# The last layer of a four-layer graph network: fetch, softmax and sums of the attention in one stage, by blocks of 112 edge tiles

## The reference

```python
def _L3_gnn_ref(x, W_u, b_u, W_v, src, dst):
    s_u = x @ W_u.T + b_u
    s_v = x @ W_v.T
    e = s_u[src] + s_v[dst]
    e = jnp.where(e >= 0, e, 0.2 * e)
    m = jax.ops.segment_max(e, dst, num_segments=n_nodes)
    e_exp = jnp.exp(e - m[dst])
    denom = jax.ops.segment_sum(e_exp, dst, num_segments=n_nodes)
    probs = e_exp / denom[dst]
    xh = x.reshape(n_nodes, head_dim, num_heads)
    msg = xh[src] * probs[:, None, :]
    out = jax.ops.segment_sum(msg, dst, num_segments=n_nodes)
    return out.reshape(n_nodes, dim)
...
h = jnp.maximum(_layernorm(x, axis=-1), 0.0)
x = x + _L3_gnn_ref(h, L3_gnn_W_u, L3_gnn_b_u, L3_gnn_W_v, src, dst)
```

## Time and profile before

| what | us |
|---|---|
| median of 3 runs | 10575.17 |
| lowest and highest run | 10565.06, 10585.32 |
| profiled execution, its time | 10629.75 |
| profiled execution, span from first to last instruction | 10628.0 |
| of it: w_uv and T4 | 8391 to 8495 |
| fetch of the last layer | 8495 to 9783 |
| softmax, two halves | 9783 to 9889, 9889 to 9996 |
| sums, with 14 us of opening | 9996 to 10583 |
| division, residual, output | 10583 to 10628 |

### The profile page before, as it was taken

One profiled execution on the slowest core, in us unless ns is written; L12 is line 12 of the kernel. 1 busy time (PEld: TensorE's weight loads), 2 busy tenths in 40 slices (PEclk: granted clock), 3 DMA queues, 4 the chain that ended last, 5 costly groups with the idle time before them and its releaser, 6 DMA issues. The chain is left out here.

```text
span 10628.0 us, 131026 instructions
## 1 busy us (share of the span) xinstructions
PE 5936.1 (56%) x24674; PEld 4756.4 (45%) x24675; DVE 4831.8 (45%) x13494; ACT 2018.0 (19%) x5480; POOL 5350.6 (50%) x5364
## 2 busy tenths in 40 slices
PE   4788886674656666645554454454455633222376
PEld 2687775553544444433333343333343432222254
DVE  6344446776544444435554233343333411112777
ACT  2111111783322222200000000010000300000276
POOL 3555552000068888876665666646666056664000
PEclk9777877997877777766666677777777655555699
DMA  4554556563067777754444333323333156665265
GB/s 148 163 158 157 166 160 208 181 200 106 2 113 105 104 105 105 104 120 142 142 142 130 91 89 91 89 82 87 91 90 90 60 165 196 188 195 151 77 200 181
DMA packets 848105, 1375.07 MB, mean 129 GB/s; under 512 B 112503, under 2 KB 501429, under 8 KB 847749
## 3 DMA queue, kind: packets, MB, share of 16 engines
q0 software_dynamic: 315328, 634.04, 27.1%
q1 hardware_dynamic: 398452, 575.30, 16.7%
q10 hardware_dynamic: 133968, 161.50, 4.8%
HBM read 949.47 MB, written 420.93 MB: 129 GB/s over the span
## 5 line engine op out<-in xcount | busy, mean ns | idle before, releaser
L1028 POOL DMA_INDIRECT regionB<-table,gather_rows x2352 | 2283.5, 971 | 1400.9 <-POOLq L1025 765.4
L1028 POOL DMA_INDIRECT regionC<-table,gather_rows x1568 | 1508.6, 962 | 861.2 <-issue 453.4
L1760 POOL DMA_INDIRECT scatter_sums<-regionC,idx x880 | 1383.7, 1572 | 306.2 <-issue 247.5
L1128 PE MATMUL ps_p<-regionB,hot 128*128 x3520 | 998.5, 443 | 846.4 <-DVE regionC L1189 511.6
L1128 PEld LDWEIGHTS ps_p<-regionB,hot 128*128 128x128 f32 x3520 | 782.9, 226 | 1035.6 <-issue 903.7
L1496 PE MATMUL ps_p<-regionA 128*128 128x266 f32 (+1 forms) x3520 | 848.4, 394 | 336.1 <-PEq L1491 216.2
L1128 PE MATMUL ps_p<-regionC,hot 128*128 x1760 | 621.7, 498 | 561.2 <-issue 487.5
L1965 PE MATMUL psS<-dst_scores,regionA 128*128 x1760 | 393.3, 362 | 897.3 <-PEq L1963 616.8
L1496 PEld LDWEIGHTS ps_p<-regionA 128*128 128x128 f32 x3520 | 653.2, 190 | 531.1 <-DVE regionC L974 194.2
L1965 PEld LDWEIGHTS psS<-dst_scores,regionA 128*128 128x128 f32 x1760 | 383.6, 330 | 907.1 <-issue 907.1
L1128 PEld LDWEIGHTS ps_p<-regionC,hot 128*128 128x128 f32 x1760 | 419.6, 249 | 763.3 <-issue 704.1
(11 more groups left out here) (309 smaller groups left out, 8503.1 us busy)
## 6 DMA issues: line engine op xcount, KB each, us to landing
regionA<-edge_rows SPq DMA_DIRECT2D x880, 256.0 KB, 3.3
edge_rows<-regionB SPq DMA_DIRECT2D x196, 512.0 KB
edge_rows<-regionC SPq DMA_DIRECT2D x392, 256.0 KB
regionC<-srcrow_d SPq DMA_DIRECT2D x220, 256.0 KB
scatter_sums<-zero_rows ACTq DMA_DIRECT2D x8, 6400.0 KB, 41.6
regionA<-scatter_sums ACTq DMA_DIRECT2D x49, 1024.0 KB
regionB<-table,gather_rows POOLq DMA_INDIRECT x2352
regionB<-rrow_d ACTq DMA_DIRECT2D x110, 256.0 KB
```

Source lines behind the costliest of these rows:

```text
L1028: g.indirect_dma_start(out=rows_of(b * per + j), out_offset=None, in_=table, in_offset=bass.IndirectOffsetOnAxis(ap=idx[:, column:column + ...
L1128: x = te.matmul(ps[(u.c * VG + j) % NB], hot[:, b, 2 * j + k, :], at_tile(G, slot[j] * 2 + k), start=k == 0, stop=k == 1)
L1760: g.indirect_dma_start(out=scat, out_offset=bass.IndirectOffsetOnAxis(ap=idx[:, b, j:j + 1], axis=0), in_=sums[:, b, j, :], in_offset=None ...
```

## The change

`attention_in_blocks` takes the place of `attention_fetch3`, both calls' work of `segment_softmax`, and `attention_sum('a3')`. The 98 groups are cut into 7 blocks of BG = 14 groups (BT = 112 edge tiles). While the groups of block c + 1 are fetched, one in each slot n, block c goes through the softmax in slots k = 0 to 4 (k = n mod 14) and through its 14 units of sums in the slots from k = 4 on. After the last slot the last block's softmax and the units 84 to 109 follow alone.

- **Softmax by blocks.** All 8 heads at once, 112 tiles on 112 partitions. `state` carries the running maximum of the segment that crosses a block's end. If the next block raises it, `settle` scales the weights of the block before on that node's edges and the one row of sums of that node by `factor`.
- **Ring and order on SP.** The ring has 4 groups and lies in B; slots are given back two groups later. `rows_in` moves from ACT's queue to SP's, ahead of keep(n) and release(n - 2).
- **Reloads.** `back` moves from SP's queue to ACT's, with 2 buffers in place of 3, and stands in ACT's order ahead of `more` of the unit before. It waits for `s_stored` (the block's rows are in DRAM) and `back_free`.
- **Region B.** x is put away in DRAM beside `ln_stats` (7 DMAs of 896 KB) and brought back at the start of the final phase, whose addition waits for it.
- Programs are written out slot by slot; before, DVE's loop over slots was rolled by 6 and the loops over units too. The zeroing of the sums stands ahead of the first hots. Targets relative to the tile (`rel`) are negated in place.

```diff
-        def attention_fetch3(LG, SV, rows_room, T_room):
-            R3 = 6
+        def attention_in_blocks(LG, SV, acc, acc_flat, ring_room, work_room):
+            R3 = 4
+            BG = 14
+            BT = BG * GS
+            NBL = ET // BT
+            LB2 = 2
...
+            def slots():
+                for n in range(NG3):
+                    c, k = n // BG - 1, n % BG
+                    units = [c * BG + i for i in range(BG) if k >= 4 and 4 + i * (BG - 4) // BG == k] if c >= 0 else []
+                    yield n, c, k, units
...
+                        for u in range(AHEAD + 1):
+                            rows_in(u)
+                        for n in range(NG3 + 2):
+                            if n + AHEAD + 1 < NU:
+                                rows_in(n + AHEAD + 1)
+                            if n < NG3:
+                                keep(n)
+                            if n >= 2:
+                                release(n - 2)
...
+                        def back(u):
+                            b = u % LB2
+                            pair = of_visits(a, pair_of, u * VG, load_pairs, PAIRS - 1)
+                            a.wait_ge(s_stored, min(NG3, (u // BG + 1) * BG))
+                            a.wait_ge(back_free[b], 1)
+                            a.sem_inc(back_free[b], -1)
+                            for j in range(VG):
+                                a.dma_start(GL[:, b, j, :], Eb[bass.ds(pair[j], 1), :, :].rearrange('a p c -> p (a c)')).then_inc(s_back_in[b], 16)
...
+                        def unit(u):
+                            if u + 1 < NU and (u + 1) % BG or u + 1 >= NBL * BG and u + 1 < NU:
+                                back(u + 1)
+                            more(u)
+                        for n, c, k, units in slots():
+                            if stages(c, k):
+                                stage(c, k)
+                                if k == 4:
+                                    back(c * BG)
+                            for u in units:
+                                unit(u)
...
+                            for j in range(VG):
+                                te.wait_ge(aux_full[b], 1)
+                                te.sem_inc(aux_full[b], -1)
+                                if j == VG - 1:
+                                    te.sem_inc(back_free[u % LB2], 1)
...
+                        for n, c, k, units in slots():
+                            if stages(c, k):
+                                stage(c, k)
+                            for u in units:
+                                multiply(u)
+                            if n + AHEAD + 1 < NU:
+                                scores(n + AHEAD + 1)
...
+                        zero_acc(v, acc_flat, NB)
...
+                            for h in range(H):
+                                back_ = BW[0:BT, h % 2, :]
+                                v.tensor_tensor_scan(FW[0:BT, h, :], f, RL[0:BT, h, :], -BIG, ALU.add, ALU.max)
+                                done(v.tensor_tensor_scan(back_[:, ::-1], b_[:, ::-1], RL[0:BT, h, ::-1], -BIG, ALU.add, ALU.max))
+                                v.tensor_copy(ends[0:BT, 0, h:h + 1], FW[0:BT, h, P - 1:P])
+                                done(v.tensor_copy(ends[0:BT, 1, h:h + 1], back_[:, 0:1]))
+                                v.tensor_tensor(FW[0:BT, h, :], FW[0:BT, h, :], back_, ALU.max)
...
+                        for n, c, k, units in slots():
+                            if stages(c, k):
+                                if k == 4 and c:
+                                    turn(c * BG - 1)
+                                stage(c, k)
+                            for u in units:
+                                scale(u)
+                                if u % BG:
+                                    turn(u - 1)
+                            if n + AHEAD + 1 < NU:
+                                hots(n + AHEAD + 1)
+                            if n + AHEAD < NU:
+                                scores_in(n + AHEAD)
+                            logits(n)
...
-        ln_stats(B256)
+        ln_stats(B256, put_away)
...
-            attention_fetch3(LG3, SV, C, A)
-            segment_softmax(LG3, LG3[:, :, :], HEADS3, (A, C))
             ACC3 = tiles(C, WT)
-            attention_sum('a3', LG3, HEADS3, False, [], 0, ACC3, C[:, 0:NT * WT], A)
+            attention_in_blocks(LG3, SV, ACC3, C[:, 0:NT * WT], B, A)
...
+                            v.wait_ge(s_x[u.val], 32)
                             v.tensor_tensor(x, x, acc[:, :, 0:D], ALU.add).then_inc(own_v, 1)
...
+                        bring_back(sp)
```

More of the change, by code:

```diff
@@ L1425, in attention_fetch0 @@
             s_used.base += NV
+            for b in range(RG0):
+                s_rows[b].base += 16 * EG * len(range(b, NEG, RG0))
         LB = 3
@@ L1927, in _ @@
                             sp.sem_inc(free3[b], 1)
-                        behind = R3 // 2
-                        for t_ in turns(sp, NG3, R3, behind, written_out=True):
-                            if t_.has(0):
-                                keep(t_.at(0))
-                            if t_.has(behind):
-                                release(t_.at(behind))
+                        for u in range(AHEAD + 1):
[7 more added lines that the diff above has]
+                                release(n - 2)
                         for b in range(R3):
@@ L1953, in _ @@
+                        for k in range(5):
+                            stage(NBL - 1, k)
+                        back((NBL - 1) * BG)
+                        for u in range((NBL - 1) * BG, NU):
+                            unit(u)
                     @block.tensor
@@ new lines, in _ @@
+                        for u in range(AHEAD + 1):
+                            scores(u)
+                        for n, c, k, units in slots():
[5 more added lines that the diff above has]
+                                scores(n + AHEAD + 1)
+                        for k in range(5):
+                            stage(NBL - 1, k)
@@ new lines, in shift @@
+                        def shift(c):
+                            v.wait_ge(factors_ready, c + 1)
+                            if c:
+                                v.tensor_scalar(mask[:, :], psT[1][:, P:P + BT], bounds[:, 0, c:c + 1], None, ALU.is_equal)
+                            done(v.tensor_copy(carry[0:BT, :, :], psT[1][0:BT, 0:2 * H].rearrange('p (k h) -> p k h', h=H)))
+                            v.sem_inc(weighed, 1)
+                            for k, m in ((0, first), (1, final)):
+                                for h in range(H):
+                                    x = v.scalar_tensor_tensor(out=FW[0:BT, h, :], in0=m[0:BT, :], scalar=carry[0:BT, k, h:h + 1], in1=FW[0:BT, h, :], op0=ALU.add, op1=ALU.max)
+                                done(x)
+                            done(v.tensor_tensor(RL[0:BT, :, :], RL[0:BT, :, :], FW[0:BT, :, :], ALU.subtract))
+                            v.sem_inc(shifted, 1)
@@ new lines, in stage, with unit @@
+                        def stage(c, k):
+                            if k == 1:
+                                masks_and_scans(c)
+                            if k == 2:
+                                carries(c)
+                            if k == 3:
+                                shift(c)
+                            if k == 4:
+                                settle(c)
+                        def unit(u):
+                            scale(u)
+                            if u:
+                                turn(u - 1)
@@ L2019, in _ @@
[L2019 to L2026 removed]
+                                scores_in(n - 1)
+                        begin()
@@ L2027, in _ @@
+                        turn((NBL - 1) * BG - 1)
+                        for k in range(5):
+                            stage(NBL - 1, k)
+                        for u in range((NBL - 1) * BG, NU):
+                            scale(u)
+                            if u > (NBL - 1) * BG:
+                                turn(u - 1)
+                        turn(NU - 1)
                         for b in (0, 1):
```

342 lines of the change are left out of this document (273 added, 69 removed).

## The result

The changed kernel takes 10315.47 us (median of 4 runs, 10306.07 to 10341.74) where the kernel before takes 10572.9: a ratio of 0.9759, 95% interval 0.9738 to 0.9781, 257 us less. A second comparison gave 0.9763 (0.9742 to 0.9784). The forecast was 10240, its range 10010 to 10460.

The account below looks back on a forecast made before the run. Three last-layer stages in a row on different engines, 2088 us, were taken as the bound; merged, 130 + 150 + 1164 + 50 + 247 = 1741, 347 less, plus 13 outside: 10296 profiled, 10240 median, range 10010 to 10460.

Parts of the forecast that it names:

- Opening, 130: Start of the merged stage: first 14 rounds of hots and scores unchanged at 119 us, plus zeroing of the sums, 10.8 us.
- Block 0, 150: First block's fetch with no unit beside it: 14 slots, ten or more groups left, 102 to 167 us, upper part taken.
- Six blocks, 194 each: Blocks with fetch and units: slots 0 to 3 45 us, slot 4 8, first reloads 8, 14 units 133; 1164 us in all.
- rival A: The unit's chain does not close and DVE decides: blocks of 175 us, last units 5.2 each, time 10015; chance 0.15.
- A unit, 9.5: Chain per unit: PE's first three visits 2.9, ACT's four issues 2.6, its hots and weights 4.0 us; before, 5.2.
- The last softmax, 50: Last block's softmax with no fetch beside it: 29 us of DVE with PE and ACT steps between, 50 us.
- Outside, 13: Putting x away beside the statistics, 8 us, and bringing it back in the final phase, 5 us; 0 to 38 possible.
- the first: Sign: ACT-queue reloads start when PE ends the previous unit's third visit; units stand 9 to 10 us apart, above all the last 26.
- the second: Sign: the first four slots of a block take about 45 us, a block 194.
- B: DVE's hold at the scores is paid again every slot, 5.9 us, 578 in all: 10818; chance of slower 0.09, a part 0.09.
- C: POOL sets the pace because DVE's products and additions push it back by their whole length: block 202 us, 10288; chance 0.05.
- D: A wait in a cycle of the queues serializes softmax and fetch: blocks of 194 + 60, 10600, same or slower; chance 0.04.

## Why the prediction was right, and where not

**Sign and size.** 257 us less for 335 forecast, inside the range. The mechanism was the forecast's: stages of different engines laid over each other, and a unit slower than before. The forecast for the profiled execution, 10296, came nearer to its 10306 than the working deserves: the two profiled executions are 324 us apart, but 45 of these lie ahead of the last layer's layernorm (8371 and 8325 us), where the kernels are the same. From there to the end it is 278 us, for 334 forecast.

**Opening, 130.** It took 106, from 8450 to the first logits at 8556, and 100 from the first gather, where the 119 of before begin. The zeroing of 10.8 us is in it, so the rounds of hots and scores were faster than the 119 of before; I took that row as fixed.

**Block 0, 150.** 156 from 8556 to 8712. Its rows before (102 to 167) bounded it well, and DVE's hold at the scores is in it, 75.9 us in 8 waits:

```profile
DVE logits L2181 <- DVEq L2177: 75.9, 8, 23.0
```

**Six blocks, 194 each.** 216: this is the term that was too small, 132 us in all. By the starts of the logits, slots 0 to 3 took 51 us for 45 and the ten slots with units 165 for 149. The timelines split the 165 further: 17 from the last logits of slot 3 to the block's first product, for 8 + 8; 4 from there to PE's first unit, which the sum had left out; 130 for the 13 steps from unit to unit, 10.0 each for 9.5; and 14 from the last unit's start to the block's last logits, for 9.5. So the units stood about as far apart as the chain said, but not for its reasons, and that is in part luck: its first link is 1 to 1.6 us here and not 2.9, its four issues 3.3 us on average and not 2.6 (2.2 on the chip without the hold), and gaps of 1 to 2 us in all were not in it. With the 7.7 of the end in place of 9.5 the forecast's own rule would have failed: 14 × 7.7 = 108 is less than DVE's 114, which is rival A's block of 175.

The step that failed is "A block is 45 + 8 + 8 + 133", because the work of the fetch and of DVE (the 4.1 us a slot, the 45) stands in it without any wait, and so do rival A's 175: with the reloads on SP a block takes 200, and without any unit 175. "POOL's 14 groups are hidden too" held, since POOL waited 410.3 us for a slot in the six blocks; it did not set the pace in the kernel without units either, while the hold was there. That the difference is the hold is shown for the kernel without units, whose blocks take 175 to 179 with it and 145 without, and for slots 0 to 3, which took 44 us without it in the kernel of doubled products, for 51, and 47 to 48 in the kernels without units, for 54 to 68. For the slots with units it is argued from there and from the slower issues; no kernel with single products ran on the chip without the hold.

**A unit, 9.5.** At the end it was 7.7, so the last 26 took 199 for 247. The term that failed is the first of its three, "PE's first three visits (2.9)": the buffer is given back 0.8 us after the unit begins. I had named a PE that runs ahead as the lower end (8.7) but kept 2.6 for the issues, which take 1.84, so the measured unit lies below the whole range of 8.7 to 10.5.

**The last softmax, 50.** 48.

**Outside, 13.** About 11. The final phase is 49 us for 45, in which the addition of x waits 2.73 us once, and from the layernorm's start to the first gather it is 7 us longer; these 7 stand in the 106 of the opening too, whose window begins 7 us before the first gather. By the profiled run:

```profile
10262.59 2.03 DVE L2689 TENSOR_TENSOR regionB<-regionB,regionC 128x1792 f32<-128x1792 f32 x1 [2.73 <-DMA regionB<-x_kept]
```

The errors have both signs: 6 × 22 too little, 24 + 48 too much, 6 too little at block 0 and 2 too much at the softmax, so 1741 became 1805. That the sum is off by 64 us and not by more is partly that they cancel.

**The signs.** Of the six, the first failed in both its halves (reloads start 0.8 us after the unit begins, and the last units stand 7.7 us apart, though those in the blocks stand 10.0), and of the second the block (216; the first four slots took 51). The others came, roughly: POOL busy 803 us in the stage for 770, DVE's wait for scores 0.4 us a slot in the six blocks (5.4 in block 0), a DMA share of 0.70 in the blocks, a granted clock of 0.67.

**Rivals.** A (5.2 a unit, 10015) is not the changed kernel, but nearly what its end becomes with the reloads on SP; the blocks do not follow. B (slower) did not come, though its mechanism did. C: gathers took 1008 ns for 970 in the blocks, 4%, as beside DVE in the first layer. A full block by each of DVE's operations would have shown as gathers longer by them, and with the products doubled and DVE busy 889 of 1306 us POOL was busy 722 of them, against 670 for the same gathers beside a DVE busy 304, both on the second chip: 8%, where DVE was busy 585 us more. The Trainium skill (SBUF — State Buffer, Who interferes with whom) says that a DVE instruction with two SBUF inputs, as the products are, contends with a GpSimd instruction that reads SBUF, not with one that only writes it. Whether a gather reads SBUF for any length of time no run here shows; the 8% is far from a full block. D did not come: softmax and fetch overlap.

## What to carry to other kernels

Overlap pays what the engines leave free, less what the merged queues make wait for each other: here 283 us of stage time from a merge in which no engine is over 53% busy. Before DMAs are moved to the queue of a computing engine, ask what that engine has behind them: a reload that waits for a buffer, ahead of the work that its own release depends on, closes a chain, and moving it to SP's queue gave 179 us more. A kernel should be timed without one of its parts before the rest is costed: the floor of fetch and softmax could not be read from busy times.

## What the runs showed of the hardware

- Waits of DVE for PE during bursts of gathers cost 262 to 278 us in 979 us on two chips, and 2 us in 872 on another; the kernel before took 10662 and 10587 us on the former and 9521 on the latter, and the 784 gathers of the first layer lay within 1442 us in the first comparison and 1051 on the last-named chip. Register loads in the two engines' programs are not the cause (266.9 us without, 277.8 with); it stays open.
- In the changed kernel, beside these waits, register instructions (L179) on DVE's and ACT's queues lasted up to 0.9 and 0.7 us in the first comparison and 1.4 us on the third chip, where on the second, without the waits, all of them took 0.12 and 0.10; PE's took 0.095 everywhere.
- PE's queue runs ahead of its products: a semaphore that stands before the last of four visits was given 0.8 us after the first began, where a unit's products last 3.8.
- Issuing four DMAs of 256 KB from ACT took 1.84 us at the end, where little else ran. Beside gathers and stores it took 3.3 us on average on a chip with the waits (the slowest eight 12.01) and 2.2 on the one without, so it is not the traffic alone.
